# Self-attention's products with V: bursts of eight for bursts of four, and a ring of twelve tiles that takes in the transposed x

## What is computed

```python
attn = jnp.einsum('bhqd,bhkd->bhqk', query, key) / scale
attn = jax.nn.softmax(attn, axis=-1)
out = jnp.einsum('bhqk,bhkd->bhqd', attn, value)
```

## Time and profile before

| | |
|---|---|
| Times of three runs | 1750.33, 1752.8 and 1753.03 us, median 1752.8 |
| The profiled execution | 1750.27 us, its span 1748.5 us |
| PE busy | 1545.2 us, 88% of the span |
| DVE busy | 1232.0 us, 70% |
| ACT busy | 862.5 us, 49% |
| POOL busy | 405.4 us, 23% |
| PE line 2024 (products with V in self-attention) | 2048 records, 274.3 us |
| PE line 1986 (transposed scores) | 1024, 344.2 us |
| PE line 1904 (scores for the maxima) | 1024, 311.7 us |
| DVE line 1465 (maxima) | 512, 601.7 us, 1218 ns each |
| ACT line 1151 (exponentials, both attentions) | 1184, 652.3 us, 599 ns each |

### The profile page before, as it was taken

How to read it: one execution, slowest core, us unless ns; L and a number is a source line. 1 busy time by engine, 2 the same in 40 slices (tenths; PEclk the granted TensorE clock), 3 DMA queues, 4 the chain that set the end, 5 groups by cost and what they waited for, 6 DMA issues and landing times. The chain is left out here.

```text
span 1748.5 us, 25995 instructions
## 1 busy us (share of the span) xinstructions
PE 1545.2 (88%) x9190; PEld 737.6 (42%) x9198; DVE 1232.0 (70%) x2551; ACT 862.5 (49%) x1611; POOL 405.4 (23%) x529
## 2 busy tenths in 40 slices
PE   7599998897999888989998989899986778999992
PEld 2222224544232255342222554322224436888872
DVE  5588854886888857888887677888865636664442
ACT  3167784353777733537777344477762231111121
POOL 5220001600200015002000250120000303666663
PEclk9699999898999998999999989899997888999997
DMA  6400001544100016350000172300002014555595
GB/s 186 124 12 1 1 2 37 153 97 104 37 1 1 1 37 183 72 135 1 1 2 29 37 191 67 105 1 2 1 1 72 23 50 123 110 111 115 111 257 120
DMA packets 101133, 118.72 MB, mean 68 GB/s; under 512 B 20365, under 2 KB 91021, under 8 KB 99853
## 3 DMA queue, kind: packets, MB, share of 16 engines
q1 hardware_dynamic: 85804, 95.81, 19.2%
q0 software_dynamic: 14208, 19.94, 6.5%
q10 hardware_dynamic: 992, 1.32, 0.3%
HBM read 65.62 MB, written 31.35 MB: 55 GB/s over the span
## 5 line engine op out<-in xcount | busy, mean ns | idle before, releaser
L1151 ACT ACTIVATE pT<-banks 128x512 f32<-128x512 f32 x1184 | 652.3, 599 | 290.5 <-PE banks L1986 165.1
L1465 DVE TENSOR_REDUCE nmf<-banks 128x1 f32<-128x1024 f32 x512 | 601.7, 1218 | 111.0 <-PE banks L1904 110.2
L1986 PE MATMUL banks<-qst,kst 99*128 99x512 bf16 x1024 | 344.2, 386 | 6.3 <-DVE nmf L1465 6.3
L1904 PE MATMUL banks<-kst,qst 96*128 96x512 bf16 x1024 | 311.7, 386 | 31.2 <-DMA qst<-oT 20.0
L2024 PE MATMUL banks<-pT,V 128*32 128x512 f32 x2048 | 274.3, 607 | 15.5 <-ACT oT L1139 12.3
L1986 PEld LDWEIGHTS banks<-qst,kst 99*128 99x128 bf16 x1024 | 96.1, 97 | 276.3 <-ACT pT L1151 173.2
L896 POOL CAST nmp<-nmf 128x16 bf16<-128x16 f32 x64 | 12.6, 196 | 774.1 <-issue 708.7
L1904 PEld LDWEIGHTS banks<-kst,qst 96*128 96x128 bf16 x1024 | 94.6, 99 | 152.2 <-DVE nmf L1465 44.6
L1321 ACT ACTIVATE kst<-banks 128x512 f32<-128x512 f32 x64 | 38.1, 597 | 204.7 <-PE banks L2350 204.6
L948 POOL DMA_INDIRECT acc_rows<-kst,tok_s x64 | 103.4, 1615 | 45.7 <-DMA acc_rows<-kst,tok_s 17.3
L1430 DVE STREAM_TRANSPOSE head_blocks<-oT 128x512 f32<-128x512 f32 x64 | 45.1, 705 | 89.5 <-ACT oT L1139 89.5
(11 more groups left out here) (244 smaller groups left out, 2168.2 us busy)
## 6 DMA issues: line engine op xcount, KB each, us to landing
qst<-q_parts SPq DMA_DIRECT2D x36, 256.0 KB, 5.1
kst<-k_parts SPq DMA_DIRECT2D x36, 256.0 KB, 7.8
qst<-in_w SPq DMA_DIRECT2D x16, 512.0 KB, 4.7
qxs<-in_w SPq DMA_DIRECT2D x16, 512.0 KB, 4.9
qst<-oT SPq DMA_DIRECT2D x60, 128.0 KB, 2.5
qxs<-oT SPq DMA_DIRECT2D x48, 128.0 KB, 2.5
xb<-in_x SPq DMA_DIRECT2D x4, 1024.0 KB, 6.8
x_rows<-z SPq DMA_DIRECT2D x4, 1024.0 KB, 8.8
```

The costliest lines, as they stand in the source:

```text
L1151: act.activation(pT[:, n % RING_P, :], PS[:, banks[what, n], :], ACT.Exp, scale=scale).then_inc(s_ex, 1)
L1465: dve.tensor_reduce(nmf[:, m % 2, j, t:t + 1], scores.rearrange("p a n -> p (a n)"), AX.X, ALU.max, negate=True).then_inc(s_smu, 1)
L1904: ins = pe.matmul(pair[:, half, :], qst[0:KQ, h, t * P:(t + 1) * P], kst[0:KQ, h, half * N:(half + 1) * N], start=True, stop=True)
L1986: ins = pe.matmul(ps, kst[0:KM, head, kc * P:(kc + 1) * P], qst[0:KM, head, cols], start=True, stop=True)
```

## The change

`BURST_SELF = 2 * TILES` makes self-attention's bursts eight products long: two blocks of keys one after the other, behind one wait for the exponential of the eighth unit. Cross-attention keeps four. `LAG` stays 3. The ring has twelve tiles for self-attention, eight for cross-attention, and exponential n of self-attention waits for av n - 12. `xT` is no longer a tensor of its own but a view of tiles 8 to 11. No instruction of work is added or removed.

```diff
+RING_SELF = 12
+BURST_SELF = 2 * TILES

 def burst_end(av, st_group):
-    return av + min(TILES, st_group - av % st_group) - 1
+    burst = BURST_SELF if st_group == ST_SELF // NG else TILES
+    return av + min(burst, st_group - av % st_group) - 1
+def ring_slot(n, cross):
+    return n % (RING_P if cross else RING_SELF)
...
-        xT = sb("xT", [P, C, S])
-        pT = sb("pT", [P, RING_P, N])
+        pT = sb("pT", [P, RING_SELF, N])
+        xT = pT[:, RING_P:RING_SELF, :].rearrange("p r n -> p (r n)").rearrange("p (c n) -> p c n", c=C)
...
-                        if n0 + n >= RING_P:
-                            act.wait_ge(s_pu, b * ST_ALL + n0 + n - RING_P + 1)
-                        act.activation(pT[:, n % RING_P, :], PS[:, banks[what, n], :], ACT.Exp,
+                        ring = RING_P if n0 else RING_SELF
+                        if n0 + n >= ring:
+                            act.wait_ge(s_pu, b * ST_ALL + n0 + n - ring + 1)
+                        act.activation(pT[:, ring_slot(n, n0 > 0), :], PS[:, banks[what, n], :], ACT.Exp,
...
-                        if k % TILES == 0:
+                        if k % (TILES if cross else BURST_SELF) == 0:
                             made = b * ST_ALL + u0 + burst_end(n, per) + 1
```

More of the change, by code:

```diff
@@ L388, in decoder_block @@
         heads_by_token = z[:, :, :].rearrange("p t d -> p (t d)").rearrange("p (n k) -> p n k", k=P)
-        xT_blocks = xT[:, :, :].rearrange("p c n -> p (c n)").rearrange("p (j n r) -> p n j r", j=TILES, r=V32)
+        xT_blocks = pT[:, RING_P:RING_SELF, :].rearrange("p c n -> p (c n)").rearrange("p (j n r) -> p n j r", j=TILES, r=V32)
         xb = sb("xb", [P, T, D])
@@ L2023, in attention @@
                             kc, j = divmod(k, TILES)
-                            ins = pe.matmul(av[V32 * j:V32 * (j + 1), :], Vf[:, kc, (g * G + j // HALVES) * VD:(g * G + j // HALVES) * VD + V32], pT[:, n % RING_P, :],
+                            ins = pe.matmul(av[V32 * j:V32 * (j + 1), :], Vf[:, kc, (g * G + j // HALVES) * VD:(g * G + j // HALVES) * VD + V32], pT[:, ring_slot(n, cross), :],
                                             start=(kc == 0), stop=(kc == T - 1), tile_position=(0, V32 * j),
@@ L2027, in attention @@
                         elif k < TILES:
-                            ins = pe.matmul(av[V32 * k:V32 * (k + 1), :], Vx[:, g * G + k // HALVES, :], pT[:, n % RING_P, :],
+                            ins = pe.matmul(av[V32 * k:V32 * (k + 1), :], Vx[:, g * G + k // HALVES, :], pT[:, ring_slot(n, cross), :],
                                             start=True, stop=False, tile_position=(0, V32 * k),
@@ L2033, in attention @@
                                 rows = slice(V32 * j, V32 * j + SKR)
-                                ins = pe.matmul(av[V32 * j:V32 * (j + 1), :], Vr[rows, g, :], pT[rows, n % RING_P, :],
+                                ins = pe.matmul(av[V32 * j:V32 * (j + 1), :], Vr[rows, g, :], pT[rows, ring_slot(n, cross), :],
                                                 start=False, stop=True, skip_group_check=True,
```

## The result

| | before | after |
|---|---|---|
| Median of the runs | 1752.91 us (4) | 1786.61 us (4; 1785.82 to 1790.34) |
| Ratio | | 1.0194, interval 1.0177 to 1.0211 |
| Profiled execution, its span | 1750.27 us, 1748.5 | 1786.50 us, 1784.7 |
| Mean granted clock | .943 | .938 |
| PE busy on the products with V | 274.3 us | 248.3 us |

The bursts of eight save PE 26 us of busy time on their own line, and the kernel is 33.7 us slower. The groups of the page's part 5 show the saving, and that DVE's work did not grow (601.7 us before).

The account below looks back on a forecast made before the run. PE sets the middle's pace (97% busy), tied to DVE and ACT through few banks. Batch 0's +6.65 and three times +7.35 give +28.7 us: 1779 for the profiled execution, 1782 as median; range 1766 to 1800.

Parts of the forecast that it names:

- start: Batch's first burst stands behind eleven units, not seven: -1.9 us in batch 0 (between 0 and that), -.2 in the others.
- first units: Three maxima to two units, DVE the bound: intervals 7.04 against 6.51 twice, 7.95 against 7.35; +1.65 us a batch.
- middle: 21 intervals, each .22 us longer as PE waits for DVE's maxima, less savings at six group boundaries: +1.9 us a batch.
- last maximum: Interval around a batch's last maximum: a unit waits for the fourth maximum, so the burst starts at 7.75; +.3 us.
- tail: After the last maximum: bursts 4.88 us apart in batch 0, +3.8; 5.60 apart in the others, held by counts, +2.8.
- last burst: End of each batch: the burst follows the last exponential uncovered, 1.88 us for 1.00; +.9.
- rival (1): Switches alone decide, DVE and ACT covering a burst of eight: .22 us gained 31 times a batch, 1712 us; chance 5%.
- (2): Maxima don't hold PE in the middle, the rest as forecast: 37 us less, 1745 us; chance 8%.
- (3): Second four products don't follow without a gap: .12 us for each of 32 bursts a batch, +15, 1797 us; chance 16%.
- The switches: PE's changes between whole-array and 32-column products: .09 us before a burst and .10 after, about .2 a burst.
- ACT causes no wait: Middle: five exponentials from 2.31 end by 5.0 us, before the interval's last score product needs a bank.
- the wait for the emptied bank: Group boundaries: the first burst's wait for ACT to empty bank 7, with late weights .47 us, goes; six times in the middle.

Follow-up runs that it names:

- half maxima: Kernel before and changed kernel, each with row maxima over the first 512 of 1024 scores: 1735.23 us with bursts of four, 1738.83 with bursts of eight.
- the ring alone: Changed kernel with its twelve tiles and xT inside them, but bursts of four: 1754.08 us, ratio 1.0007 to the kernel before.
- fours in the tail: Changed kernel with bursts of eight up to unit 208 of each batch and of four from there on: 1771.93 us, ratio 1.0110.
- the pair moved: Changed kernel with each interval's fourth pair, from unit 40 on, behind the last unit before the burst: 1783.64 us, ratio 1.0162.
- fours later: Changed kernel with bursts of four, lag six instead of three, bank 7 emptied six units after a group's end, division two later: 1748.56 us, ratio .9971.

## Why the prediction was right, step by step

1786.6 lies in the range of 1766 to 1800 and in the forecast's own of 1768 to 1797, 4.6 over the 1782. Self-attention in the two profiled executions, from a batch's first unit to its last product with V, after minus before; a stage ends at the start of the last product of a burst of eight, and of the same product before, and the length that a burst gained (1.86 - 1.00 = .86) is taken from the start and put at the last burst, as in the forecast:

| us | forecast, batch 0 / others | batch 0 | 1 | 2 | 3 |
|---|---|---|---|---|---|
| start | -1.9 / -.2 | -.16 | +.21 | +.56 | -.28 |
| first units (three intervals) | +1.65 | +1.58 | +.96 | +.96 | +.96 |
| middle (21 intervals) | +1.9 | +1.99 | +1.98 | +1.97 | +1.99 |
| last maximum | +.3 | +1.72 | +.28 | +.29 | +.28 |
| tail | +3.8 / +2.8 | +4.03 | +2.97 | +2.97 | +1.63 |
| last burst | +.9 | +.86 | +.86 | +.86 | +.86 |
| sum | +6.65 / +7.35 | +10.01 | +7.26 | +7.60 | +5.44 |

That the sum, 30.3, came so near the forecast's 28.7 is in part luck: the starts came out 2.8 over, the last maximum of batch 0 1.4 over, the first units 2.1 under and batch 3's tail 1.2 under. The middle and the distances between bursts are no luck of that kind.

**Which of the cases.** Bursts 5.88 apart in the middle (forecast 5.90), 7.02, 7.01, 7.93 at first (7.04, 7.04, 7.95; batch 0's first, at half clock in part, is 7.55), 7.71 around the last maximum (7.75; batch 0 below), 4.89 and 5.57 in the tails (4.88, 5.60), 1.86 a burst (1.88): the forecast, and neither rival (1) or (2), which needed 5.5, nor (3), which needed a burst of 2.0. The switches were priced rightly: by distances a burst of eight takes 1.86 where two of four take 2.00, and one step of .31 into a burst becomes one of .22, together .23 for the .22 of the forecast. (The 26 us less on PE's line agree with 128 x (.09 + .10) = 24, but hold modelled ends.) The Trainium skill's rule (TensorEngine Tiling (Array Packing), Key Properties) is that TensorE drains at a change of tiling mode and not at a change of tile. The trace agrees: the second four, on the same four tiles, follow at .86 for 1.00. The rule tells nothing of the engines that had been fed in between, and there the loss arose.

**The middle.** That the third and fourth pair wait for the first two maxima is shown by the experiment with half maxima, for the plain intervals. My statement that ACT causes no wait holds for these alone, and by a narrow margin: moving the fourth pair brought ACT's wait out at once.

**The boundary.** The forecast was that the wait for the emptied bank goes. It went. By the forecast's terms an interval with a boundary (3.31 + 2.84 = 6.15 before) becomes 6.15 + .22 - .47 + .1 = 6.00, and one with a turn (3.00 + 2.84 = 5.84 before) becomes 5.84 + .22 - .1 = 5.96; they take 6.03 and 5.95. The sizes are right and the reason is not: half maxima leave 6.03 as it is and take .04 from 5.95, so that the .22 for DVE and the .1 for its division are not what is paid there. At a boundary it is ACT, late by the time in which it emptied bank 7 (239.95, .59). These are eleven of the 21 intervals, and that they fit is luck.

**The first units** are smaller in batches 1 to 3. I took batch 0's 6.51 before for all four; in the others one of those intervals was 3.46 already and not 2.84, so .6 of the loss was there before the change.

**The start of batch 0** is the term that was mis-sized: -1.9 forecast (between 0 and that), -.16 measured. The windows of after (columns as in the earlier trace rows), there and behind batch 0's last maximum:

```profile
92.00:96.00 4.00, 4.00 (x12) 1.11 (x14) 3.46 (x3) 2.28 (x4) 4.00 (x2) 0.50 0.34 59
...
250.00:253.40 3.40, 3.40 (x17) 0.63 (x17) 0.00 (x0) 0.60 (x1) 0.83 (x4) 0.50 0.00 0
```

and of before:

```profile
82.00:92.00 10.00, 8.98 (x25) 2.02 (x26) 5.00 (x5) 4.26 (x9) 8.77 (x11) 0.50 0.20 46
92.00:96.00 4.00, 3.76 (x21) 1.15 (x20) 3.48 (x3) 2.52 (x5) 4.00 (x1) 1.00 0.33 62
```

I had put the first burst past the stretch at half clock (1.2 GHz). That stretch ended at about 92 before and lasted past 96 after, so that the burst of eight still took 2.39 (95.28 to 97.67) for 1.86, and the units ahead of it stayed slow. In the profiled executions the stretch is 10.2 us long before the change and with the ring alone, and 13.7 after it, in the run with fours in the tail, in that with the pair moved and in that with fours later, in all of which the first burst comes later; with half maxima it is 6.8 and 10.2. Why, no run tells.

**Batch 0's last maximum.** It is 1.4 over there since the clock was at half (1.2 GHz) from 250.0 to 253.4, right behind a wait of 1.66:

```profile
249.94 0.57 PE L1995 MATMUL banks<-qst,kst 99*128 99x512 bf16 x1 [1.66 <-DVE nmf L1474]
250.44 3.38 PE L2033 MATMUL banks<-pT,V 128*32 128x512 f32 x16
```

The burst then took 3.31 (to 253.75) for 1.86; no step of mine had it. Batch 3's tail shows +1.63 for the opposite reason: there the kernel before had such a stretch at half clock behind its own last maximum, and its first interval of the tail was 3.62 for 2.16.

**What stays open.** Self-attention gives 30.3 of the 36.2 between the two profiled executions. The other 5.9 lie between the batches and at the ends, in stages that the change doesn't touch. The mean clocks of the two executions differ (.943 and .938), and the ring alone shows that moved xT doesn't cost it; which stretch falls to half clock, and why, I did not test. Between medians the difference is 33.7, so part of the 5.9 may be spread between executions.

## What to carry to other kernels

A longer burst on one engine saves its switches, but the engines that it feeds through a few buffers then stand for as much of the burst as the buffers don't cover: walk one cycle from the burst's start, and see whether what the buffers hold (here two maxima, 2.36 us, of the four that a cycle needs) lets the others come back in time. Where a stage ends on a loop through the burst's own last input, as in the tails, each product more in a burst adds to the loop its own time (.22) and a step of the feeding engine (.48). The wait at a group's boundary goes with a longer lag and bursts of four too: there a group got .24 faster, and with bursts of eight .39 slower.

## What the runs showed that was not expected

A stretch of 3.4 us at half clock that begins around the end of the wait for the last maximum (1.58 before, 1.66 after) is no steady companion of that wait. In the changed kernel it came in batch 0 and not in batches 1 to 3, where the same wait stands and the burst behind it takes 1.86. Before, it came in batch 3 alone, with the ring alone in batches 1 and 3, with fours in the tail in batches 0, 2 and 3, and with the pair moved in batches 0 and 1.

Two bursts of float32 products on column tiles, one directly behind the other in the same four tiles, cost .86 for the second (1.86 - 1.00), less than the first and without a gap. That was the forecast (.88), but no row of the kernel before had shown it.
